# Bidirectional scan kernel: residual DMAs moved up GpSimd's queue, the scan input's minimum for tiles 1 to 8 on GpSimd, and another order at the end

## What is computed

```python
decay = exp(-exp(w)) * (0.5 + 0.5 * tf)          # one value per batch and channel
ek = exp(minimum(k, 30)); ekv = ek * k
# forward and backward scans over time, for ekv (num) and ek (den):  a = a * decay + input
euk = exp(minimum(u + k, 30))
num = nf + nb - ekv + euk * k
den = df + db - ek + euk
y = sigmoid(x) * num / maximum(den, 1e-8) * (0.8 + 0.2 * tf)
out = x + y @ binarized(weight).T + bias         # weight: +-1 times the row's mean |w|
```

## Time and profile before

| | us |
|---|---|
| median of 3 runs (543.01 to 545.19) | 544.06 |
| the profiled execution, its own time | 544.33 |
| its span, first to last instruction | 542.6 |
| VectorE busy | 504.8 (93%) |
| ScalarE busy | 378.4 (70%) |
| TensorE matmuls busy | 363.8 (67%) |
| GpSimd busy | 362.3 (67%) |

### The profile page before, as it was taken

One profiled execution on the slowest core, in us unless ns is written; L12 is line 12 of the kernel. 1 busy time (PEld: TensorE's weight loads), 2 busy tenths in 40 slices (PEclk: granted clock), 3 DMA queues, 4 the chain that ended last, 5 costly groups with the idle time before them and its releaser, 6 DMA issues.

```text
span 542.6 us, 5454 instructions
## 1 busy us (share of the span) xinstructions
PE 363.8 (67%) x1803; PEld 224.1 (41%) x1803; DVE 504.8 (93%) x385; ACT 378.4 (70%) x415; POOL 362.3 (67%) x194
## 2 busy tenths in 40 slices
PE   2233333322578786786786798778799888759996
PEld 1123333312335544444443454554455444524442
DVE  4999999999999999999999999999999999994593
ACT  2849688585859697796969696978889595953100
POOL 0157676667677877777877788877877879873200
PEclk9975655556698798798899878878899999779999
DMA  6745677777633798788899788888779998982942
GB/s 192 196 136 175 195 185 182 206 200 194 155 97 102 148 194 173 163 206 160 157 192 194 153 177 182 185 185 180 180 134 193 216 200 148 195 169 65 185 164 117
DMA packets 125778, 92.64 MB, mean 171 GB/s; under 512 B 2844, under 2 KB 117560, under 8 KB 125752
## 3 DMA queue, kind: packets, MB, share of 16 engines
q0 software_dynamic: 30720, 33.56, 39.2%
q1 hardware_dynamic: 92952, 57.70, 36.0%
q10 hardware_dynamic: 2080, 1.05, 0.7%
HBM read 58.74 MB, written 16.78 MB: 139 GB/s over the span
## 4 chain that ended last, share of the span: by engine, by line
DVE 59%; issue 22%; PE 11%; POOL 5%; DVEq 1%; ACT 1%; DMA 1%; SPq 0%; ACTq 0%
DVE pair L683 25%; DVE pair L704 9%; DVE wkv L740 7%; DVE own L722 6%; POOL wkv L345 5%; DVE pair L721 4%; DVE pair L715 4%; PE sT L420 3%; PE kT L420 3%; PE yT L420 2%; PE prod L420 1%; DVE euk L745 1%; PE cols L420 1%; DVE y_start L696 1%; DMA cond<-in_cond_dram 1%
## 5 line engine op out<-in xcount | busy, mean ns | idle before, releaser
L385 PE MATMUL prod<-acts,sgn 128*128 128x512 f16 x768 | 181.3, 390 | 4.3 <-ACT orow L618 4.0
L704 DVE TENSOR_TENSOR_SCAN pair<-cols,y_start,pair 128x1024 f32<-128x1024 f32 x64 | 150.1, 2346 | 1.1
L363 PE MATMUL kT<-ident,k_nat 128*128 128x128 f32 x256 | 52.1, 371 | 147.1 <-DVE own L722 147.1
L683 DVE TENSOR_TENSOR_SCAN pair<-cols,pair 128x1024 f32<-128x1024 f32 x64 | 142.8, 2272 | 0.0
L326 POOL TENSOR_TENSOR wkv<-euk,rec 128x1024 f32<-128x1024 f32 x31 | 73.1, 2357 | 84.0 <-ACT rec L558 84.0
L385 PEld LDWEIGHTS prod<-acts,sgn 128*128 128x128 f16 (+1 forms) x768 | 77.4, 101 | 90.2 <-issue 9.6
L363 PEld LDWEIGHTS kT<-ident,k_nat 128*128 128x128 f32 x256 | 42.1, 192 | 158.5 <-issue 157.9
L556 ACT ACTIVATE rec<-euk,lnb 128x1024 f32<-128x1024 f32 x32 | 36.8, 1150 | 84.9 <-DVE euk L745 84.8
L335 POOL TENSOR_TENSOR wkv<-wkv,rec 128x1024 f32<-128x1024 f32 x31 | 72.9, 2350 | 18.1 <-ACT wkv L591 18.1
L345 POOL TENSOR_TENSOR wkv<-wkv,pair 128x1024 f32<-128x1024 f32 x31 | 74.1, 2392 | 11.5 <-DVE wkv L740 10.1
L301 POOL TENSOR_TENSOR acts<-wkv,rec 128x1024 f16<-128x1024 f32 x31 | 73.2, 2363 | 9.5 <-ACT rec L567 9.5
(11 more groups left out here) (88 smaller groups left out, 502.2 us busy)
## 6 DMA issues: line engine op xcount, KB each, us to landing
x_nat<-in_x_dram SPq DMA_DIRECT2D x32, 512.0 KB, 6.9
pair<-own POOLq DMA_DIRECT2D x32, 512.0 KB, 4.7
k_nat<-in_fside_BxSxS_dram SPq DMA_DIRECT2D x30, 512.0 KB, 3.5
o_nat<-in_x_dram POOLq DMA_DIRECT2D x24, 512.0 KB, 9.1
out_dram<-o_nat SPq DMA_DIRECT2D x24, 512.0 KB, 5.0
y_fm<-in_L_ffn_weight_dram SPq DMA_DIRECT2D x8, 512.0 KB, 5.7
x_end<-in_x_dram SPq DMA_DIRECT2D x6, 512.0 KB, 5.1
x_end<-in_L_ffn_bias_dram POOLq DMA_DIRECT2D x6, 512.0 KB, 6.0
```

The lines of the kernel that those rows point to most:

```text
L363: ins = pe.transpose(dst(q), what(q), one)
L385: ins = pe.matmul(prod[:, h, :], view[:, c, m % CT * P:m % CT * P + P], acts[:, part, m // CT % 2 * CT + c, h * H:(h + 1) * H], start=(par ...
L683: dve.tensor_tensor_scan(buf, d, buf, 0.0, ALU.mult, ALU.add).then_inc(st["F" + kind], 1)
L704: dve.tensor_tensor_scan(buf[:, ::-1], d, buf[:, ::-1], y_start[:, i:i + 1], ALU.mult, ALU.add)\
```

## The change

1. **Minimum on GpSimd.** For tiles 1 to 8 (`by_pool`) ScalarE's exponential gets the bias ln(scl), so that it yields ek * scl, and GpSimd takes the minimum with `ceil` = E30 * scl (`ceiling`, its own instruction, between `chk` and `inv`). VectorE's L715 goes for these tiles. For this ScalarE makes `exp_e(n+1)` before `two`, and the high half's value back (`high_back`) and `exp_u` after it. ln(scl) is made once, at the start: on ScalarE a logarithm and an exponential of 128 x 32, on VectorE one instruction for `ceil` ahead of the first tile, and two of 128 x 32 in step 0 that correct the logarithm to first order.
2. **Residual and bias DMAs** stand right behind the numerator's DMA on GpSimd, ahead of `chk`, in all steps.
3. **The end.** ScalarE empties units 47 and 46 (`evac`, `y_copy`) in step 30 and not in step 31, and copies the last unit before `two` of step 31. TensorE makes early piece 8 over 5 tiles and not 6, ahead of its wait for tile 29's low half; the sixth is added at the end.
4. VectorE's wait for `base` of tile n-2 moves from L715 to the row behind it.

```diff
     def cleared(n):
-        return 0 if n < LAG else made(n) - 1 if n < N - 1 else 2 * LAST
+        return 0 if n < LAG else made(n) - 1 if n < N - 2 else 2 * LAST
...
+        def by_pool(n):
+            return 1 <= n < LAG
...
@@ GpSimd @@
+            def ceiling(n, p):
+
+                done(pool, "expE", n)
+                pool.wait_ge(s_lnscl, 1)
+                pool.tensor_scalar(ek[p], ek[p], ceil[:, n:n + 1], None, ALU.min).then_inc(st["clamp"], 1)
...
                     pool.dma_start(ekv[1 - p], own[1 - p][:, :], accum_op=ALU.add).then_inc(num_in[1 - p], 16)
+                residuals(summed(n))
+                if 3 <= n <= TT:
+                    biases(n - 3)
+                if mid:
 
                     done(pool, "rec", n - 1)
                     done(pool, "lo", n - 3)
                     pool.tensor_tensor(W, euk[1 - p][:, :], R, ALU.mult).then_inc(st["chk"], 1)
+                if by_pool(n + 1):
+                    ceiling(n + 1, 1 - p)
                 first = n % CT == 1
                 if low and first:
                     low_half(n - 2, p)
-                if not first:
-                    residuals(summed(n)[:1])
...
-                residuals(summed(n) if first else summed(n)[1:])
-                if 3 <= n <= TT:
-                    biases(n - 3)
@@ TensorE, the end @@
+            done(pe, "yc", 2 * LAST - 1)
+            across(8, bank[4], range(CT - 3), True, True).then_inc(st["early"], 1)
             done(pe, "lo", N - 3)
             for v in range(4):
                 across(v, bank[v], range(CT - 3, CT - 2), False, False)
-            done(pe, "yc", 2 * LAST - 1)
-            across(8, bank[4], range(CT - 2), True, True).then_inc(st["early"], 1)
             s_turn(N - 1)
@@ ScalarE @@
+                if by_pool(n):
+
+                    act.wait_ge(s_lnscl, 1)
+                    act.activation(ek[p], kT[:, :], ACT.Exp, bias=lnscl[:, n:n + 1]).then_inc(st["expE"], 1)
...
+            act.wait_ge(s_scl, 1)
+            act.activation(lnscl[:, :], scl[:, :], ACT.Ln).then_inc(s_ln, 1)
+            act.wait_ge(s_ln, 1)
+            act.activation(lnerr[:, :], lnscl[:, :], ACT.Exp, scale=-1.0).then_inc(s_back, 1)
...
-                    halves(n - 2, p)
+                    high_half(n - 2, p)
+                if by_pool(n + 1):
+                    exp_e(n + 1, 1 - p)
+                elif low:
+                    high_back(n - 2, p)
                 if out:
                     clear(cleared(n - 1), made(n - 1))
+                if n == N - 1:
+                    y_copy(2 * LAST - 1)
                 if mid:
 
                     done(act, "chk", n - 1)
                     act.activation(wkv[1 - p][:, :], wkv[1 - p][:, :], ACT.Identity,
                                    scale=-HI_SCALE * LO_GAIN, bias=two[:, 0:1]).then_inc(st["two"], 1)
...
-            y_copy(2 * LAST - 1)
             early_out(0)
@@ VectorE @@
+            link(dve.tensor_scalar(ceil[:, :], scl[:, :], E30, None, ALU.mult))
...
-                done(dve, "expE", n)
-                done(dve, "base", n - 2)
-                dve.tensor_scalar(E, E, E30, scl[:, col], ALU.min, ALU.mult).then_inc(st["clamp"], 1)
+                if not ceil_pool:
+
+                    done(dve, "expE", n)
+                    dve.tensor_scalar(E, E, E30, scl[:, col], ALU.min, ALU.mult).then_inc(st["clamp"], 1)
...
+                if first:
+
+                    dve.wait_ge(s_back, 1)
+                    link(dve.tensor_tensor(lnerr[:, :], lnerr[:, :], scl[:, :], ALU.mult))
+                    dve.scalar_tensor_tensor(lnscl[:, :], lnerr[:, :], -1.0, lnscl[:, :], ALU.add, ALU.add)\
+                       .then_inc(s_lnscl, 1)
```

More of the change, by code:

```diff
@@ L127, in bi_wkv_binary_ffn @@
         oscale = sb("oscale", [P, N])
+        lnscl = sb("lnscl", [P, N])
+        lnerr = sb("lnerr", [P, N])
+        ceil = sb("ceil", [P, N])
         lnb = sb("lnb", [P, 1])
@@ L140, in bi_wkv_binary_ffn @@
         csum_ps = prod[:, 1, 0:B]
-        s_par, s_cond, s_id, s_rows, s_wub, s_csum, s_every, s_ew, s_eew, s_ecs, s_const, s_ucol, s_dve, s_osc = (
+        s_par, s_cond, s_id, s_rows, s_wub, s_csum, s_every, s_ew, s_eew, s_ecs, s_const, s_ucol, s_dve, s_osc, s_scl, s_ln, s_back, s_lnscl = (
             sem(a) for a in ("s_par", "s_cond", "s_id", "s_rows", "s_wub", "s_csum", "s_every", "s_ew", "s_eew", "s_ecs",
-                             "s_const", "s_ucol", "s_dve", "s_osc"))
+                             "s_const", "s_ucol", "s_dve", "s_osc", "s_scl", "s_ln", "s_back", "s_lnscl"))
         k_in, w_in, num_in = ([sem(f"{a}{p}") for p in range(2)] for a in ("k_in", "w_in", "num_in"))
@@ L190, in over @@
                     yield q
+        def by_pool(n):
+            return 1 <= n < LAG
         def flags(n):
-            return dict(wt=int(n < CT), nxt=int(n + 1 < N), nxt3=int(n + 3 < N),
+            return dict(ceil_pool=int(by_pool(n)), wt=int(n < CT), nxt=int(n + 1 < N), nxt3=int(n + 3 < N),
                         mid=int(1 <= n), low=int(2 <= n), out=int(LAG <= n))
@@ L251, in _, with step @@
             load_x(1)
-            def step(n, p, wt, nxt, nxt3, mid, low, out):
+            def step(n, p, ceil_pool, wt, nxt, nxt3, mid, low, out):
                 if wt:
@@ L503, in _ @@
                     done(pe, "res", v - 8)
-                tiles = range(CT - 2, CT) if v < 6 or v in (8, 9) else range(CT - 1, CT) if v < 8 else range(CT)
+                tiles = range({6: CT - 1, 7: CT - 1, 8: CT - 3}.get(v, CT - 2) if v < 10 else 0, CT)
                 across(v, bank[v % 8], tiles, v >= 8, True).then_inc(st["nat"], 1)
@@ L518, in _, with exp_e, exp_u @@
             act.activation(ecs[:, :], csum_ps, ACT.Exp, scale=-1.0).then_inc(s_ecs, 1)
-            def exps(n, p):
+            def exp_e(n, p):
                 done(act, "kT", n)
                 done(act, "den", n - 2)
-                act.activation(ek[p], kT[:, :], ACT.Exp).then_inc(st["expE"], 1)
+                if by_pool(n):
+                    act.wait_ge(s_lnscl, 1)
+                    act.activation(ek[p], kT[:, :], ACT.Exp, bias=lnscl[:, n:n + 1]).then_inc(st["expE"], 1)
+                else:
+                    act.activation(ek[p], kT[:, :], ACT.Exp).then_inc(st["expE"], 1)
+            def exp_u(n, p):
                 act.activation(euk[p][:, :], kT[:, :], ACT.Exp, bias=ucol[:, bass.ds(n, 1)])\
@@ L558, in inverse, with high_half, high_back @@
                 act.activation(rec[p][:, :], rec[p][:, :], ACT.Exp, scale=-1.0).then_inc(st["rec"], 1)
-            def halves(n, p):
+            def high_half(n, p):
                 if n >= 2 * CT:
                     done(act, "prod", n // CT * 2 * CT - 2 * CT - 1)
-                high = acts[:, 0, n % (2 * CT), :]
-                act.mul(high, wkv[p][:, :], 1.0 / LO_GAIN).then_inc(st["hi"], 1)
+                act.mul(acts[:, 0, n % (2 * CT), :], wkv[p][:, :], 1.0 / LO_GAIN).then_inc(st["hi"], 1)
+            def high_back(n, p):
                 done(act, "hi", n)
-                act.mul(rec[p][:, :], high, LO_GAIN).then_inc(st["hib"], 1)
+                act.mul(rec[p][:, :], acts[:, 0, n % (2 * CT), :], LO_GAIN).then_inc(st["hib"], 1)
             def early_out(i):
@@ L575, in _, with step @@
             act.wait_ge(s_ucol, 2)
-            exps(0, 0)
+            exp_e(0, 0)
+            exp_u(0, 0)
+            act.wait_ge(s_scl, 1)
+            act.activation(lnscl[:, :], scl[:, :], ACT.Ln).then_inc(s_ln, 1)
+            act.wait_ge(s_ln, 1)
+            act.activation(lnerr[:, :], lnscl[:, :], ACT.Exp, scale=-1.0).then_inc(s_back, 1)
             act.dma_start(k_nat[0][:, :, :], tile_of(k, 2)).then_inc(k_in[0], 16)
-            def step(n, p, wt, nxt, nxt3, mid, low, out):
+            def step(n, p, ceil_pool, wt, nxt, nxt3, mid, low, out):
                 if mid:
@@ L592, in step @@
                                    scale=-HI_SCALE * LO_GAIN, bias=two[:, 0:1]).then_inc(st["two"], 1)
-                if nxt:
-                    exps(n + 1, 1 - p)
+                if by_pool(n + 1):
+                    if low:
+                        high_back(n - 2, p)
+                    exp_u(n + 1, 1 - p)
+                elif nxt:
+                    exp_e(n + 1, 1 - p)
+                    exp_u(n + 1, 1 - p)
                 if out:
@@ L627, in _ @@
             done(act, "base", N - 2)
-            halves(N - 2, 0)
+            high_half(N - 2, 0)
+            high_back(N - 2, 0)
             early_out(1)
             act.wait_ge(st["last_base"], 1)
-            halves(N - 1, 1)
+            high_half(N - 1, 1)
+            high_back(N - 1, 1)
         @block.vector
@@ L674, in _ @@
             link(dve.tensor_scalar(scl[:, :], scl[:, :], S_MIN, None, ALU.max))
+            dve.sem_inc(s_scl, 1)
             link(dve.reciprocal(back[:, :], scl[:, :]))
@@ L719, in step @@
                 done(dve, "clamp", n)
+                done(dve, "base", n - 2)
                 done(dve, "expU", n)
```

## The result

The changed kernel takes 559.21 us (median of 4 runs, 559.07 to 560.08) against 543.87 before (also 4 runs): ratio 1.028, 95% interval 1.026 to 1.031. I had forecast 535.6. Its profiled execution took 560.08 us, its span is 558.2 (before 542.6).

What follows compares the result with a forecast made beforehand. The prediction took VectorE, busy 93% of the span, to bound the kernel. From 544.33 us, +0.4 (start) - 1.0 (minimum) - 3.2 (steps 27 and 29) - 4.9 (end) = -8.7 gave 535.6 us; range 531.0 to 544.0.

Steps and rivals of the forecast that it cites:

- The start: Small operations on 128 x 32 elements before the steady steps; two on VectorE in step 0 lie on the path: +0.4 us.
- The minimum moved: Tiles 1 to 8: VectorE loses L715, but the longer chain through GpSimd hands most back; sum -1.0 us.
- X: Time of the minimum on GpSimd, in no row: taken as 1.2 us, between bounds of 0.75 and 2.35.
- The walk: Chain through ScalarE, GpSimd and VectorE in steps 2 to 7, ending with `den`: a step lasts 15.36 us.
- D: Start of the count in a step: the end of the denominator `den`, 85.17 us for step 5.
- Step 8: Last step without L715 on VectorE, with no minimum to make on GpSimd: its 0.75 us stays saved.
- the rule of `den`: VectorE's `den` ends no earlier than 1.09 us after GpSimd's `base`; both have two inputs in SBUF.
- Residual DMAs moved: Residual and bias DMAs run between the numerator's DMA and `chk`; outside steps 27 and 29 no gain or loss counted.
- my slower rival: VectorE's L715 and L689 wait for GpSimd's descriptor writing to end: 32.1 us more, 567.7 us; chance 14%.
- Steps 27 and 29: The second residual DMA no longer stands ahead of `base`, so `den` ends earlier: -1.58 us each, -3.2 for both.
- The end: After the last `den`: the last logarithm starts 4.81 us earlier, the last 28 matmuls 5.4 earlier; sum -4.9 us.
- The "no change" rival: The minimum on GpSimd is slow, at 2.35 us: 7.9 us more, 543.5 us; chance 13%.

Runs made afterwards that it cites:

- min_half: The kernel before with only the minimum moved to GpSimd, taken over 512 of the 1024 columns: 548.09 us (one run).
- min_none: The kernel before with only the minimum's move and ScalarE's new order, the minimum itself left out: 545.51 us (one run).
- dmas_wait_den: The kernel before with only the residual and bias DMAs moved up, GpSimd waiting for the denominator's end before issuing residuals: 541.48 us (one run).
- dmas_only: The kernel before with only the residual and bias DMAs moved behind the numerator's DMA: 551.59 us, ratio 1.013.
- best2: The kernel before with the new order at the end, and residual DMAs moved up behind a wait for the denominator: 535.68 us, ratio 0.985.
- dmas_one_port: The kernel before with only the residual and bias DMAs moved up, and VectorE's clamp written in its slow form: 554.52 us (one run).

## Why the prediction was wrong

Point by point, forecast and measured:

- *The start*: +0.4; measured +0.3 to +0.4. Right.
- *The minimum moved*: -1.0; measured +11.5. **The step that failed is the time X of the minimum: "Upper bound: the two-input operations' 2.35 us", and "I take 1.2, half of the two-input time, since half of the reads go."** It took 2.84 us, so the one-input operation was dearer than the two-input ones, and that half of the reads would halve the time rested on no row. Of the 12.5 us between forecast and measurement 7.9 lie between X = 1.2 and 2.35, the rest above my bound. The row of the one-input operation, 0.29 us for 128 columns, pointed to 2.3 us, nearer than my 1.2; but it too is another operation, and it is near by luck in part, for 2.5 ns a column and 0.3 fixed would make 0.6 us of 128 columns. The walk itself held: X + 14.16 as long as the minimum sets the start of `inv`. With X = 2.84 that is D + 6.07 + 2.84 + 2.31 + 2.35 + 2.34 + 1.09 = D + 17.00, measured 17.06; with 1.56 (`min_half`) 15.72, measured 15.79; with no minimum `two` sets it, 15.22, and `min_none` measured 15.27.
- *Step 8*: -0.75; measured 0.0. Not seen: the small `oscale` operation, two inputs in SBUF, stands behind the scans and ends with GpSimd's `inv`. Timelines, VectorE before and after, then GpSimd after:

```profile
138.41 1.02 DVE L731 TENSOR_TENSOR oscale<-asum,gain 128x32 f32<-128x32 f32 x1
```

```profile
149.47 1.80 DVE L781 TENSOR_TENSOR oscale<-asum,gain 128x32 f32<-128x32 f32 x1
```

```profile
148.88 2.34 POOL L351 TENSOR_TENSOR wkv<-wkv,rec 128x1024 f32<-128x1024 f32 x1 [1.26 <-ACT wkv L625]
```

  VectorE came 0.8 us earlier and waited 0.8 us longer. It is the rule of `den` again, and I had applied it to one row only.
- *Residual DMAs moved*: 0 in the 21 steps; measured +0.58 each, 12.2 in sum. **The second step that failed is that the forecast put the clamp's meeting with the DMA's issue at nothing.** My reasons against a price, that the descriptors may be written in a short part of the time and that GpSimd can wait instead, rested on no row. This was my slower rival, to which I gave 14%. Its mechanism was right in that the issue holds the clamp; its price was too high: it let VectorE wait to the end of the issue, 1.36 us, and the bias DMAs hold L689 as well, which they hardly do (0.68 us beside one).
- *Steps 27 and 29*: -1.58 each; measured -1.55 in the changed kernel, but there it is another sum, and the number agrees by luck: 0.58 goes to the clamp (it is in the 12.2 above as well), and `den` is free at 1.23, not held near 1.8. With the clamp undisturbed (`dmas_wait_den`) it is -1.59, and `den` at 1.76: the mechanism was right.
- *The wait for `base` moved (part 4)*: not costed; +1.0.
- *The end*: -4.9; measured -5.0. Right.

So the direction was lost on two numbers, X and the clamp's 0.58 us, each of which alone cost more than the gains of steps 27, 29 and the end together (8.1 us). The "no change" rival had the slow minimum right in kind and priced it at 7.9 us, against 12.5 measured: even my worst case for that term was bounded by rows of another kind of operation.

## What to carry to other kernels

Moving work from a busy engine to an idle one pays only if the chain back through the idle one gets no longer: here the moved operation needed another order on ScalarE, which made GpSimd's operations 1.24 us late, and so even with the moved operation at no cost at all the step gained 0.03 us. Price an operation that no row shows by the rate of the nearest row, leave room above it, and do not cap it by rows of another kind: the nearest rate gave 2.3 us here, the chip took 2.84. When a DMA's issue on GpSimd has to stand beside a VectorE row in the fast form, let the VectorE row start first: a wait for the operation ahead of it turned +7.6 us (`dmas_only`) into -2.9 (`dmas_wait_den`, one run), and `best2` keeps that gain over five runs.

## What the hardware showed that I had not expected

- GpSimd's fp32 minimum with a scalar takes 2.84 us on 128 x 1024 (constant: 2.78; 512 columns: 1.56), its multiplication of two tensors 2.35. The Trainium skill ("GPSIMD Engine Reference", section 4.1, Engine selection) calls one-input work on GpSimd roughly line-rate, which I estimate at about 0.9 us here by the 1.03 cycles an element of its section 3.1, Elementwise; the measurement is three times that, and it decides.
- A VectorE `tensor_scalar` at twice the usual pace takes some 0.58 us longer if it starts just behind the start of the issue of a DMA of 1024 short rows (128x8x128), not at all if it starts first, and not in its slow form. The Trainium skill ("SBUF — State Buffer", Who interferes with whom) has the order of issue decide and the later one block fully. The runs agree in that a clamp that started first was not slowed. They don't show a full block: the clamp ended before the issue did (219.83 against 220.22), and the issue, which had started first, grew too, by 0.27 us in the mean (2.21 in `dmas_only`, 1.94 in `dmas_one_port`).
- Beside the issue of a bias DMA in the same place it was mostly the issue that grew: in `dmas_only` it took 1.36 us against 1.17 in `dmas_one_port`, while the clamp behind its start stayed at 0.75 and steps 3 to 7 grew by some 0.03 us. Why VectorE gives way beside the one DMA and hardly beside the other stays open.
- An operation on 32 columns took 1.02, 1.80 or 0.18 us, by what GpSimd was doing at the time: in the first two cases it ended within 0.05 us of the end of `inv` (139.43 and 139.38 before, 151.27 and 151.22 after), in the third GpSimd only issued a DMA.
